# One visit per kind of tile: the scores-and-values stage of a decoder layer with its TensorE work put in another order

## The reference

```
x = layernorm(x + causal_attention(x))            # 16 heads of 16, rotary q and k
x = layernorm(x + cross_attention(x, ctx))        # 77 context keys, 16 heads
x = layernorm(x + feed_forward(x))                # 256 -> 1024 (silu gate) -> 1024 -> 1024 -> 256, gelu
```

## Time and profile before

| | |
|---|---|
| median of 3 runs | 966.22 us (963.57 to 967.8) |
| profiled execution | 965.38 us, span 963.7 us |
| PE busy | 878.7 us, 91% of the span |
| DVE busy | 535.0 us, 56% |
| ACT busy | 354.5 us, 37% |
| POOL busy | 328.0 us, 34% |
| chain that ended last | PE 74%, DVE 14%, POOL 4%, issue 4%, ACT 2% |
| true steps of S, sequence 0 and 1 | start at 75.6 us and 558.0 us |
| mean granted TensorE clock | 0.958 of full |

### The profile page before, as it was taken

The page is one execution under the profiler, slowest core; times in us unless marked ns, Lnnn a source line. Parts: engine busy times, 40 slices in busy tenths (PEclk is TensorE's granted clock), DMA queues, the critical chain, the costliest instruction groups (busy, mean ns, idle before and its releaser), DMA issues.

```text
span 963.7 us, 14216 instructions
## 1 busy us (share of the span) xinstructions
PE 878.7 (91%) x5034; PEld 576.5 (60%) x5034; DVE 535.0 (56%) x1385; ACT 354.5 (37%) x746; POOL 328.0 (34%) x554
## 2 busy tenths in 40 slices
PE   5879999898999999988989899998999999999996
PEld 2544444235666667876666654443476667887885
DVE  4697888677666633145343588883366653116113
ACT  0315766464433411114111166766733342122210
POOL 4412323447300444425222233233440024335332
PEclk9867999879999999999999999998999999999998
DMA  9909101002200232325222024340000000000000
GB/s 328 311 1 387 74 2 46 23 0 76 88 1 1 68 95 102 110 75 166 88 88 88 29 94 164 133 155 2 1 2 1 2 1 1 1 1 23 1 1 23
DMA packets 23849, 68.71 MB, mean 71 GB/s; under 512 B 4401, under 2 KB 11569, under 8 KB 23601
## 3 DMA queue, kind: packets, MB, share of 16 engines
q1 hardware_dynamic: 23776, 67.77, 20.1%
HBM read 65.40 MB, written 13.63 MB: 82 GB/s over the span
## 4 chain that ended last, share of the span: by engine, by line
PE 74%; DVE 14%; POOL 4%; issue 4%; ACT 2%; SPq 1%; DMA 0%; POOLq 0%; DVEq 0%; ACTq 0%
PE bank L833 23%; PE bank L643 6%; PE bank L661 6%; PE bank L612 6%; PE bank L821 4%; DVE max_raw L1131 4%; PE bank L742 4%; DVE bank L1133 4%; PE bank L752 4%; PE bank L830 3%; PE bank L693 3%; PE bank L598 2%; PE bank L556 2%; PE bank L763 2%; POOL prob_s L1398 2%
## 5 line engine op out<-in xcount | busy, mean ns | idle before, releaser
L964 ACT ACTIVATE prob_s<-bank 128x512 f32<-128x512 f32 (+3 forms) x384 | 163.5, 497 | 91.8 <-PE bank L643 91.5
L1427 POOL TENSOR_TENSOR hid_lo_s<-act_raw_s,hid_hi_s 128x512 fp32r<-128x512 f32 x96 | 123.7, 1288 | 212.2 <-DVE hid_hi_s L1294 177.4
L612 PE MATMUL bank<-k_t_s,q_t_s 64*128 64x512 f32 (+3 forms) x384 | 138.4, 451 | 25.7 <-DVE max_raw L1133 16.4
L1398 POOL TENSOR_SCALAR_AFFINE_SELECT prob_s<-prob_s 128x128 f32<-128x128 f32 x256 | 83.1, 341 | 161.1 <-ACT prob_s L964 158.8
L1294 DVE CAST hid_hi_s<-act_raw_s 128x512 fp32r<-128x512 f32 x64 | 30.5, 477 | 193.1 <-ACT act_raw_s L1025 192.8
L1133 DVE CUSTOM_DVE_ANT_0 bank<-bank,causal_bf 128x128 f32<-128x128 f32 (+3 forms) x256 | 122.8, 509 | 15.2 <-PE bank L612 13.1
L643 PE MATMUL bank<-q_t_s,k_t_s 64*128 64x512 f32 (+3 forms) x384 | 115.7, 416 | 2.0 <-issue 1.2
L1025 ACT ACTIVATE act_raw_s<-bank,scales 128x512 f32<-128x512 f32 x64 | 43.7, 689 | 180.8 <-PE bank L833 180.8
L612 PEld LDWEIGHTS bank<-k_t_s,q_t_s 64*128 64x128 f32 x384 | 63.5, 199 | 70.3 <-DVE max_raw L1133 31.3
L643 PEld LDWEIGHTS bank<-q_t_s,k_t_s 64*128 64x128 f32 x384 | 59.1, 199 | 76.6 <-ACT prob_s L964 50.4
L1131 DVE TENSOR_REDUCE max_raw<-bank 128x1 f32<-128x512 f32 x128 | 82.3, 684 | 36.0 <-PE bank L612 36.0
(11 more groups left out here) (154 smaller groups left out, 1511.5 us busy)
## 6 DMA issues: line engine op xcount, KB each, us to landing
ring_s<-scratch SPq DMA_DIRECT2D x34, 512.0 KB, 3.2
home_s<-scratch SPq DMA_DIRECT2D x22, 512.0 KB, 6.0
checked_s<-scratch SPq DMA_DIRECT2D x3, 3584.0 KB, 21.3
ring_moved_s<-scratch SPq DMA_DIRECT2D x10, 512.0 KB, 3.2
x_t_s<-in_x_t SPq DMA_DIRECT2D x2, 1024.0 KB, 5.2
x_tok_s<-in_x SPq DMA_DIRECT2D x2, 1024.0 KB, 7.5
out<-tok SPq DMA_DIRECT2D x16, 128.0 KB, 1.7
q_t_s<-max_rows SPq DMA_DIRECT2D x64, 4.0 KB
```

What stands on the lines that cost most here:

```text
L612: mm(out[:, 0:k1 - k0], qkt(q, p, 0)[r, P * qt:P * (qt + 1)], qkt(q, p, 1)[r, k0:k1], start=True, stop=True).then_inc(S["max_mm"], 1)
L964: act.activation(prob[q][4 * (s % 2) + j][:, 0:n], S_BANK[j][:, 0:n], ACT.Exp, scale=SCALE).then_inc(S["exp_done"], 1)
L1398: pool.affine_select(out=pr, in_=pr, compare_op=ALU.is_ge, fill=0.0, base=0, pattern=[[1, P]], channel_multiplier=-1).then_inc(S["select_d ...
L1427: pt(dst[1][:, m], act_raw[q][r % 3][:], dst[0][:, m].bitcast(F32), ALU.subtract).then_inc(S["f_lo"], 1)
```

## The change

UNITS lists head half 0 ahead of half 1. In a true step TensorE's order becomes: units 0 and 1; scores 0 to 3; units 2 and 3; the round if it is a pair's last turn (k == 3); the norm products around the values as before; and last every other round (turns 0 to 2, rows, Y). In steps below 0 a quarter of the step's feed-forward products follows each unit, and rounds follow the second quarter. ACT takes all four exponentials, then the norm evacuations, and then evacuates rounds.

```diff
-UNITS = [(hh, qt, half) for qt in range(NT) for half in range(1 + qt // 4) for hh in (1, 0)]
+UNITS = [(hh, qt, half) for qt in range(NT) for half in range(1 + qt // 4) for hh in (0, 1)]
...
-        def f_products(slot, exact):
+        def f_products(slot, exact, part=0, parts=1):
             if slot is None:
                 return
-            for q, n, i in F_MM[slot]:
+            work = F_MM[slot]
+            for q, n, i in work[len(work) * part // parts:len(work) * (part + 1) // parts]:
                 f_product(q, n, i, exact)
...
+        def rounds(q, s, last_turn):
+            for kind, i, k in ROUNDS:
+                if kind == "turn" and turn_step(i, k) == s and last_turn == (k == 3):
+                    turn(q, i, k)
+                if kind == "rows" and rows_step(i) == s and not last_turn:
+                    rows(q, i)
+                if kind == "y" and y_step(i) == s and not last_turn:
+                    y_turn(q, i)
...
             units = [(p, u) for p in range(NP) for u in range(NU) if max_step(p, u) == s]
-            for j in range(4):
-                if 0 <= s < LAST:
-                    score(q, s, j)
-
-                for unit in units[j:j + 1]:
-                    max_unit(q, *unit)
-                for kind, i, k in ROUNDS:
-                    if kind == "turn" and j == 1 and turn_step(i, k) == s:
-                        turn(q, i, k)
-                    if kind == "rows" and j == 1 and rows_step(i) == s:
-                        rows(q, i)
-                    if kind == "y" and j == 3 and y_step(i) == s:
-                        y_turn(q, i)
+            if s < 0:
+                for j in range(4):
+                    for unit in units[j:j + 1]:
+                        max_unit(q, *unit)
+                    f_products(slot, exact, j, 4)
+                    if j == 1:
+                        rounds(q, s, last_turn=True)
+                        rounds(q, s, last_turn=False)
+                return
+            for unit in units[0:2]:
+                max_unit(q, *unit)
+            for j in range(4) if s < LAST else ():
+                score(q, s, j)
+            for unit in units[2:4]:
+                max_unit(q, *unit)
+            rounds(q, s, last_turn=True)
             f_products(slot, exact)
             norm_products(q, "S", s, ("yt", "proj"))
             if 0 <= s - 1 < LAST:
                 values(q, s - 1)
             norm_products(q, "S", s, ("xt", "q"))
+            rounds(q, s, last_turn=False)
...
             if 0 <= s < LAST:
-                exps(q, s, (0, 1))
+                exps(q, s, range(4))
+            norm_evacs(q, "S", s)
             for kind, i, j in ROUNDS:
                 if kind == "turn" and turn_step(i, j) == s:
                     turn_evac(q, i, j)
                 if kind == "rows" and rows_step(i) == s:
                     rows_evac(q, i)
-            if 0 <= s < LAST:
-                exps(q, s, (2, 3))
-            norm_evacs(q, "S", s)
```

## The result

The changed kernel took 1037.18 us (median of 4 runs, 1028.32 to 1047.59) and the kernel before 966.41 us. The ratio on record is 1.0667, with a 95% interval from 1.0611 to 1.0724; it leaves out the run of 1047.59 us, which fell in a slower state, and is not the quotient of the two medians. That is slower, as forecast, but by 64 us (by the ratio) to 71 us (by the medians) where 30.5 were forecast, and outside the range. The profiled execution took 1035.52 us, with a span of 1033.8.

What follows compares the result with a forecast made beforehand. True steps were taken as bound by a loop of PE units and DVE reductions; 22.0 + 6.6 + 2.7 - 1.0 - 0.7 + 0.9 = +30.5 us gave 997 us. Its own range was 988 to 1004, widened with rivals to 978 to 1009.

Steps and rivals of the forecast that it cites:

- Turns: True steps: each turn moves onto the loop between unit 3 and the next unit 0, 38 x 0.58 = +22.0 us.
- Evacuation behind the turn: Steps 5, 13, 17, 25: Y waits for ACT to empty the bank shared with the turn, +0.83 us, 8 times, +6.6 us.
- y_evac: After steps 12 and 24: the turn ahead of the next unit gives DVE's y_evac its time, -0.24 us, 4 times, -1.0 us.
- y_norm: Behind Y in five steps per sequence: DVE's y_norm delays the next first reduction, +0.27 us, 10 times, +2.7 us.
- Rows, order of units, exponentials: Rows transpose on the loop against one saved change of kind, -4 to +5 us, taken as zero; ACT's regrouping and half order nothing.
- Head: Sequence 1's head: lone units among products cost 39.3 us where units and products took 40.0, so -0.7 us.
- rival 2: Sequence 1's head: lone units far cheaper than at measured spacing, 972 us, with half of it 984; chance 0.05.
- The clock: Term of +0.9 us in the sum, for one fall of the clock brought by the new stalls.
- Rival 3: Stalls at Y bring the clock down in each of eight turn-and-Y steps, +8 x 1.2 us, 1006 us; chance 0.08.
- Rival 1: TensorE is the bound; one change of kind fewer in 50 steps saves about 0.2 us each, 956 us; chance 0.08.
- Rival 4: The turn is absorbed because the next step's unit 0 gets ahead, 966 us; chance 0.03.

Runs made afterwards that it cites:

- e1: Changed kernel with turn and rows back between scores and units 2 and 3, Y behind unit 3, ACT in its old order; ratio 1.0033.
- e4: Changed kernel with each score product of steps 0 to 32 issued twice into its bank; 1000.15 us, ratio 1.0310.
- e2: Kernel before with only the rounds moved behind the values (last turns behind unit 3) and ACT regrouped; ratio 1.0776.
- e6: Kernel before with spare DVE reductions: one in each of 38 turn steps, three in steps 5, 13, 17 and 25; ratio 1.0410.
- e9: Changed kernel with each turn of the 38 turn steps made twice, behind the values; 1037.51 us, ratio 1.0679.
- e14: Changed kernel with Y ahead of the values and each score of steps 0 to 32 issued twice; 981.66 us, ratio 1.0153.
- e3: Kernel before with one spare DVE reduction of 512 columns in each of the 38 turn steps; 1002.34 us, ratio 1.0331.

## Why the prediction was right in direction and wrong in size

The reading of the bound was right: the turn was off the loop of units and reductions, and putting it on costs its whole 0.58 us. The terms, one by one:

- **Turns, 22.0 us.** Right. Turn steps at full clock are 0.57 us longer (steps 8 and 12), and e1, which takes them off the loop again, is back at 1.0033.
- **Evacuation behind the turn, 0.83 us, 8 times.** Right within a tenth: Y starts 1.50 us behind the turn in step 13, and the forecast had 1.41. PE waits for ACT there in all eight steps, 0.8 us each.
- **y_evac, -0.24 us, 4 times.** Right: 0.81 us before, 0.53 after, so -0.28. With it step 13 should grow by 0.58 + 0.83 - 0.24 = 1.17 us, and it grows by 1.20.
- **y_norm, 0.27 us.** A little large, and it falls in the step behind Y: DVE starts 0.74 us behind the unit of step 14 in place of 0.57. At full clock (e4) step 14 grows by 0.81 us and step 18 by 0.75, a turn's 0.57 and 0.24 or 0.18 more.
- **Rows, order of units, exponentials, zero.** Nothing speaks against it: e1 shows 0.03 us a step for the joined kinds, and the sum below leaves little room for more.
- **Head, -0.7 us.** Measured -2.2 to the start of step 1. Waits gone, as said, and paid for in the spacing of lone units; the wait for DVE's residual sums at step 0 wasn't in the forecast. The -26 us of rival 2 were never there.
- **Together at full clock:** 22.0 + 6.6 + 2.7 - 1.0 = 30.3 us in the true steps, measured 28.9 to 31, of which the 1.8 us in step 0 of sequence 1 are the head's. The moved work is thus some 27 to 29 us.
- **The clock, +0.9 us. This is the step that failed.** No run shows that term: that the new stalls would bring one fall, at 0.9 us, was the author's estimate. The rows have step 29 at 5.15 us in sequence 0, at a clock of 0.82, and at 4.28 in sequence 1, at 1.00, and the runs show 35 to 37 us in the true steps. Some may lie between them too, but how much isn't shown: the steps behind 32 in sequence 0 took 3.8 us more at a clock of 0.74 for 0.79, with Y moved there as well. The forecast reckoned with one fall. The clock fell 8 times in true steps, and was low for 141 us in all: 102 behind these falls, and 39.5 carried in from sequence 0's head, where before it was 8.7.

Rival 3 named the clock and mis-sized it too. Of the 8 falls 6 came in a step with turn and Y or in the one behind, as it had it. The price of half clock was to be had from the earlier trace rows: 5.15 - 4.28 = 0.87 us for 2 x 0.18 x 5.15 = 1.85 us of it, 0.47 each, even above the 0.27 to 0.31 that the pairs of kernels gave. What was wrong was the amount, 2 us where 128 more came, because both the term and the rival took each fall to end with its step. The clock row of the page before spoke against that, with 6 and 7 and again 8 and 7 in slices that are neighbours, each 24 us or some seven steps long. Had the range held the case that a quarter of the true steps, some 60 us, runs at half clock, it would have reached 60 x 0.47 = 28 us higher than the likeliest value, to 1025, still just short of the runs; with half of the steps it holds them.

Rival 1 fell on e1: one change of kind less saved 0.03 us, and the loop decided as the earlier trace rows had shown. Rival 4 fell on the windows.

What sets how long the clock stays low isn't settled. e2 and e6 tell that it goes with the turn behind the values and not with idle time as such, and e4, e9 and e14 that repeated scores or turns in the steps shorten it (141 us of half clock to 14 and 80, and 78 to 5). Which property of the order does it isn't shown: each kernel that moved the turn also changed what stands next to it, and none separated the two.

## What to carry to other kernels

Find the loop first, then ask of each moved instruction whether it lands on it: windows over like steps with and without it tell its price, here 0 before and 0.57 us after. Where an edit makes TensorE's steps longer and gives it no more work, as the change and the pauses of e3 and e6 did (mean clocks of 0.894, 0.927 and 0.936 for 0.958), forecast both clock levels, with the steps' length at each and a share of the steps from none to half, and let the range hold both. A low clock is worth repair only where TensorE is on the loop: 0.27 to 0.31 us per us of half clock in the true steps, but 1.0 us for 17 in the tail of sequence 0.

## What the runs showed of the hardware

- More work took less time: 264 repeated products brought the ratio from 1.0667 to 1.0310, by a clock of 0.952 for 0.894.
- Replacing fp32 transposes by fp32r products of the same size lowered the clock, 0.894 to 0.830 and 0.958 to 0.933, with the same time per step at full clock (steps 6 to 8 take 3.83 to 3.97 us with products and 3.84 to 3.97 with transposes).
- Equal numbers of falls (8) were followed by 41 us of half clock in one order and 102 in another, with PE idle in steps at full clock for about as long in both (0.46 and 0.42 us in step 8, 1.76 and 1.42 in step 13).
- A profile's busy share doesn't show the loss: in the 39.5 us at half clock at the start of sequence 0's true steps PE is busy for 38.0.
